# A down product in quarters, attention scores in column tiles, and the second quantisation's factor on GpSimd

## What is computed

```python
def _act_quant(x):
    scale = 127.0 / jnp.clip(jnp.max(jnp.abs(x), axis=-1, keepdims=True), 0.0001, None)
    y = jnp.clip(jnp.round(x * scale), -128, 127) / scale
def _ternary_quant(w):
    s = jnp.mean(jnp.abs(w))
    wq = jnp.round(jnp.tanh(w / (s + EPS))) * jnp.arctanh(s)
def _linear_bit(x, w, g):
    return einsum('bsd,od->bso', _act_quant(_rmsnorm(x, g)), _ternary_quant(w))

x = x + xattn(_layernorm(x), ctx, mask)        # softmax over 64 context rows
u = _layernorm(x)
h = silu(_linear_bit(u, w1, g1)) * _linear_bit(u, w2, g2)   # inner width 2048
x = x + _linear_bit(h, w3, g3)
```

## Time and profile before

| what | value |
|---|---|
| median of 3 runs | 471.52 us (470.7 to 474.17) |
| the profiled execution's own time | 472.33 us |
| its span, first to last instruction | 470.5 us |
| PE busy | 409.9 us, 87% of the span |
| VectorE busy | 407.1 us, 87% |
| GpSimd busy | 341.3 us, 73% |
| ScalarE busy | 339.5 us, 72% |
| mean granted TensorE clock | 0.942 of full speed |

### The profile page before, as it was taken

The page is one execution under the profiler, slowest core; times in us unless marked ns, Lnnn a source line. Parts: engine busy times, 40 slices in busy tenths (PEclk is TensorE's granted clock), DMA queues, the critical chain, the costliest instruction groups (busy, mean ns, idle before and its releaser), DMA issues. The chain is left out here.

```text
span 470.5 us, 8445 instructions
## 1 busy us (share of the span) xinstructions
PE 409.9 (87%) x1966; PEld 197.5 (42%) x1966; DVE 407.1 (87%) x927; ACT 339.5 (72%) x607; POOL 341.3 (73%) x539
## 2 busy tenths in 40 slices
PE   8326644899999999999999999999999999999995
PEld 8102412344644464446434543445444634334432
DVE  3799576889899999999999999999999999999662
ACT  1585446986798769886988788878886796666552
POOL 0267858787777787788788787778777877878650
PEclk9756795899999999999999999999999999999998
DMA  7999901545557455745574466447654444444431
GB/s 270 396 366 421 312 16 22 135 90 114 139 148 173 90 114 143 179 88 115 165 178 89 111 182 163 90 111 189 139 129 111 91 88 91 86 94 91 90 69 45
DMA packets 110504, 67.45 MB, mean 143 GB/s; under 512 B 100752, under 2 KB 100880, under 8 KB 106768
## 3 DMA queue, kind: packets, MB, share of 16 engines
q1 hardware_dynamic: 110480, 67.19, 53.9%
HBM read 34.14 MB, written 8.39 MB: 90 GB/s over the span
## 5 line engine op out<-in xcount | busy, mean ns | idle before, releaser
L521 POOL TENSOR_TENSOR stageB<-stageB,g3b 128x512 f32<-128x512 f32 x128 | 163.8, 1285 | 46.2 <-DVE stageB L907 45.3
L1163 PE MATMUL S<-W2q,q12T 128*128 128x512 f16 x512 | 134.5, 386 | 8.9 <-DVE stageB L907 6.2
L1163 PE MATMUL S<-W1q,q12T 128*128 128x512 f16 x512 | 135.3, 388 | 0.0
L693 ACT ACTIVATE sg<-S,asc 128x512 f32<-128x512 f32 x128 | 87.5, 683 | 54.1 <-PE S L1163 49.3
L1191 PE MATMUL DN<-W3q,stageB 128*128 128x512 f16 x512 | 118.7, 386 | 7.3 <-DMA stageB<-stageB 7.3
L907 DVE TENSOR_TENSOR stageB<-sg,S 128x512 f32<-128x512 f32 x128 | 86.7, 677 | 19.9 <-ACT sg L693 10.5
L913 DVE TENSOR_REDUCE hm<-stageB 128x1 f32<-128x512 f32 x128 | 86.5, 677 | 0.2 <-POOL stageB L521 0.2
L1163 PEld LDWEIGHTS S<-W2q,q12T 128*128 128x128 f16 x512 | 49.5, 99 | 75.3 <-DVE stageB L907 13.9
L1191 PEld LDWEIGHTS DN<-W3q,stageB 128*128 128x128 f16 x512 | 49.8, 99 | 70.3 <-issue 10.8
L1163 PEld LDWEIGHTS S<-W1q,q12T 128*128 128x128 f16 x512 | 49.8, 100 | 66.3 <-issue 10.1
L685 ACT ACTIVATE stageB<-stageB,hf 128x1024 f16<-128x1024 f32 x64 | 69.8, 1140 | 4.8 <-DVE hf L933 4.8
(11 more groups left out here) (112 smaller groups left out, 430.7 us busy)
## 6 DMA issues: line engine op xcount, KB each, us to landing
xTs<-in_xT SPq DMA_DIRECT2D x8, 1024.0 KB, 7.0
X<-in_x SPq DMA_DIRECT2D x8, 1024.0 KB, 6.0
out_x<-X SPq DMA_DIRECT2D x32, 256.0 KB, 2.9
X<-in_w1T SPq DMA_DIRECT2D x4, 1024.0 KB, 12.5
stageB<-in_w2T SPq DMA_DIRECT2D x4, 1024.0 KB, 20.4
X<-in_w3T SPq DMA_DIRECT2D x4, 1024.0 KB, 9.2
ctxr<-in_ctx SPq DMA_DIRECT2D x16, 128.0 KB, 3.1
ctxc<-in_ctx SPq DMA_DIRECT2D x8, 128.0 KB, 3.9
```

The costliest lines, as they stand in the source:

```text
L521: nc.gpsimd.tensor_tensor(gh[q][:, part], hp[:, part], g3b[:, part], ALU.mult).then_inc(s_gh_made, 1)
L693: nc.scalar.activation(sg[n % 2][:, :], S1[n % 2][:, :], ACT.Silu, scale=asc[z][:, 0:1])\
L1163: mm = nc.tensor.matmul(bank[n % 2][:, :], q12T[q][:, i * KD + k, :], w[:, n, k, :], start=(k == 0), stop=(k == KD - 1))
```

## The change

Four things are changed together.

1. The down product of tile t - 2 is cut in quarters of 4 matmuls and spread over the slot: one after up chunk 0, one after chunk 1, two after chunk 2. A new semaphore `s_down_top` says that the upper half of q3T has been read, and the first transpose of the next tile waits for that instead of the whole product.
2. The scores are computed the other way round: the centred context ccT (128 x 64) is the weight, and 256 columns of x transposed are moved; even tiles go to columns 0 to 63 of the array and odd tiles to columns 64 to 127 (`tile_position`). The result lies transposed in PSUM; ScalarE copies it to the new tile `half`, and two PE transposes turn it back before the softmax.
3. stage_h_factor and worth_3 move from VectorE to GpSimd, four operations. VectorE keeps the maximum and takes the reciprocal of it directly. On GpSimd the root and the factor stand behind stage_a_mean and quantize_12 of the new row instead of before them.
4. `result` on VectorE moves from before gate 1 or 2 to between max_3(t, 0) and gate 3, and `hsc` has two buffers.

In the diff, subscripts of whole tiles and unchanged waits are dropped.

```diff
 def load_xT(a):
-    sp.wait_ge(s_scores_ps, a)
+    sp.wait_ge(s_half_ps, a)
 def transpose_3(t, h):
-    sp.wait_ge(s_down_ps, t)
+    sp.wait_ge(s_down_ps if h else s_down_top, t)
 # gpsimd
+def stage_h_root(t, z):
+    ...
+    tensor_scalar(hkk, hk, asc[z][:, 1:2], QMAX * QUANTUM / ACT_MAX_FLOOR, mult, mult)
+def stage_h_factor(t):
+    pool.wait_ge(s_h_kk, t + 1)
+    pool.wait_ge(s_h_r, t + 1)
+    ...
+    tensor_scalar(hf, hr, QMAX * QUANTUM, hkk, mult, min)
+    ...
+    tensor_scalar(ha, hm1, hkk, QMAX * QUANTUM, mult, max)
+def worth_3(t, q):
+    pool.wait_ge(s_h_a, t + 1)
+    tensor_scalar(hsc[q], ha, wc[:, 2:3], ACT_MAX_FLOOR / (QMAX * QUANTUM), mult, mult)
 slot, gpsimd:
     gain_3(t - 1, 3, (j - 1) % 2)
-    stage_h_root(t - 1, (j - 1) % NZ)
     stage_a_mean(t + 2, (j + 2) % TPB)
     quantize_12(t + 1)
+    stage_h_root(t - 1, (j - 1) % NZ)
+    stage_h_factor(t - 1)
+    worth_3(t - 1, (j - 1) % 2)
     stage_a_worth(t + 1, (j + 1) % NZ)
 # scalar
+def attention_half(a):
+    act.wait_ge(s_half_ps, a + 1)
+    nc.scalar.copy(half[:, :], R[1][:, 0:TPB // 2 * P]).then_inc(s_half_made, 1)
 slot, scalar:
 silu(t, 1, j % NZ)
 if attn and j == 0 and not first:
+    attention_half(b + 1)
     two(x_square, b + 1, 2)
 # vector
 def stage_h_top(t):
     tensor_reduce(hm1, hm, AX_X, max).then_inc(s_h_max, 1)
+    dve.wait_ge(s_h_max, t + 1)
+    reciprocal(hr, hm1).then_inc(s_h_r, 1)
 # tensor
 def attention_scores(a):
-    for j in range(TPB):
-        for k in range(KD):
-            matmul(R[1][:, j * M:(j + 1) * M], xTs[:, k, j, :], ccT[:, k, :], ...)
+    for k in range(KD):
+        for e in range(2):
+            matmul(R[1][e * M:(e + 1) * M, 0:TPB // 2 * P], ccT[:, k, :], xTs[:, k, e::2, :],
+                   ..., tile_position=(0, e * M))
+def attention_turn(a):
+    pe.wait_ge(s_half_made, a + 1)
+    for i in range(TPB // 2):
+        transpose(R[1][:, i * P:(i + 1) * P], half[:, i * P:(i + 1) * P], identf)
 slot, tensor:
 up(t, 0, q)
-down(t - 2)
+down(t - 2, 0, 1)
 up(t, 1, q)
+down(t - 2, 1, 1)
 if attn and j == 0: attention_scores(a)
 up(t, 2, q)
+down(t - 2, 2, 2)
+if attn and j == 0: attention_turn(a)
 up(t, 3, q)
```

More of the change, by code:

```diff
@@ L107, in bit_ffn_xattn @@
         identf = sb("identf", [P, P])
+        half = sb("half", [P, TPB // 2 * P])
         warm = sb("warm", [P, 4])
@@ L153, in bit_ffn_xattn @@
         hkk = sb("hkk", [P, 1])
-        ha = [sb(f"ha{i}", [P, 1]) for i in range(2)]
+        ha = sb("ha", [P, 1])
         hr = sb("hr", [P, 1])
         hf = sb("hf", [P, 1])
-        hsc = sb("hsc", [P, 1])
+        hsc = [sb(f"hsc{i}", [P, 1]) for i in range(2)]
         S1 = [ps(f"S1_{i}", [P, CH]) for i in range(2)]
@@ L597, in slot @@
                     quantize_12(t + 1)
+                if not (first and j == 0):
+                    stage_h_root(t - 1, (j - 1) % NZ)
+                    stage_h_factor(t - 1)
+                    if not (first and j == 1):
+                        worth_3(t - 1, (j - 1) % 2)
+                if not (last and j == TPB - 1):
                     if first and j == 0:
@@ L1040, in slot @@
                     stage_a_gain(t + 2)
-                if not early and j == 1:
-                    worth_3(t - 2, j % 2)
-                    result(t - 2)
                 gate(t, 1)
@@ L1052, in slot @@
                     weight_scale(2, stageA, W3f, 1, s_w3_dve)
-                if not early and j != 1:
-                    worth_3(t - 2, j % 2)
-                    result(t - 2)
                 if attn and j < 3:
                     stage_a_max(t + 2)
-                if first and j == 1:
-                    stage_h_factor(0, 0, 0)
                 gate(t, 2)
@@ L1067, in slot @@
                     weight_clip(W3f, 1, s_w3_dve, 1, s_w3_q)
+                if not early:
+                    result(t - 2, j % 2)
                 gate(t, 3)
@@ L1211, in slot @@
                     attention_ccT(a)
-                if not (first and j < 2):
-                    down(t - 2)
+                turn = not (first and j < 2)
+                if turn:
+                    down(t - 2, 0, 1)
                 up(t, 1, q)
+                if turn:
+                    down(t - 2, 1, 1)
                 if attn and j == 0:
@@ L1226, in slot @@
                 up(t, 2, q)
+                if turn:
+                    down(t - 2, 2, 2)
                 if first and j == 0:
                     attention_scores(a)
+                if attn and j == 0 and not first:
+                    attention_turn(a)
                 up(t, 3, q)
+                if first and j == 0:
+                    attention_turn(a)
                 if attn and j == 1:
@@ L1236, in _ @@
             turn_3(NT - 1)
-            down(NT - 1, True)
+            down(NT - 1, turned=True)
 def kernel(**inputs):
```

101 lines of the change are left out of this document (59 added, 42 removed).

## The result

The changed kernel takes **477.24 us** (median of 5 runs, 475.9 to 477.92) against 472.18 for the kernel before on the same chip (470.7 to 474.17): a ratio of **1.0104, interval 1.0071 to 1.0137**. It is slower by about 5 us where I forecast 11 faster; the time lies above my range. The loss is clear of the scatter, but the interval holds the 1% that I had called the least a measurement can tell. Ranges and ratios in this document are of executions at the kernel's usual granted clock; one execution further down, at a mean clock of 0.927 where the same kernel's others had 0.943 to 0.945, stands outside them.

The account below looks back on a forecast made before the run. VectorE and PE were taken to bound the middle together. Gains of 7.8 (six batches), 2.0 (batch 7), 1.2 (batch 0) and 0.2 (end) sum to 11.2 us: 460.3 on the median, range 453 to 470, the forecast's own 456 to 465.

Parts of the forecast that it names:

- What bounds before: Middle batches: VectorE (49.2 us occupied) and PE (48.3) bound together, VectorE slightly first; GpSimd occupies 42.4.
- Change 3 on GpSimd: Four one-element operations added on GpSimd: 1.3 us a slot, 5.3 a batch, raising its occupied time from 42.4 to 47.7.
- the stretch exists in each slot already: GpSimd beside VectorE's gains: stretching only moves to other operations and is already in the 42.4, so 1.3 a slot holds.
- The allowance for waits: Middle batches: 0.5 us for waits between nearly equally full engines, giving 48.2 a batch, 1.3 less than 49.50.
- my slower rival: GpSimd waits for the new row's mean, 1.35 us in three of four slots: 51.75 a batch, 481.6 us; 7%.
- Change 2 on PE: Scores on PE fall from 3.51 us to 2.3, plus 0.3 for two transposes; PE goes from 48.3 to 47.4 a batch.
- Change 1 and batch 7: Batch 7: the 1.1 us late transpose is covered by 1.7 of PE work; 2.0 of 3.3 us of waits gained.
- hf now stands behind the new row's 1.36: GpSimd's chain is late next after the transpose wait goes, as hf follows 1.36 us of the new row's quantising.
- The start and the end: Batch 0 gains 1.2 us because c comes earlier on VectorE; the end gains 0.2 as two small operations change engine.
- The rule on the shared port pair: VectorE and GpSimd block each other fully: at most 0.9 us a slot more on GpSimd; forecast kept 1.3 a slot.
- that rival: GpSimd stands for VectorE's whole 1.67 us gain pair: 51.3 a batch, 478.9 us, 3%; at half, 468.1, 5%.
- The two slower rivals: GpSimd waiting at its slot's new head (481.6 us, 7%) and standing for the whole gain pair (478.9 us, 3%).

Follow-up runs that it names:

- the first experiment: Kernel before with changes 1, 2 and 4 but the factor left on VectorE and GpSimd's order unchanged: 462.87 us, ratio 0.9789.
- the kernel with the root first: Changed kernel with the inner row's root and hkk put back ahead of the new row's mean on GpSimd: 470.22 us, ratio 0.997 to the kernel before.

## Why the prediction was wrong, point by point

**What bounds before.** Right. With changes 1, 2 and 4 alone the loop stays at 49.4, because VectorE is full. And the change did relieve VectorE: 6.4 us of waits for other engines in a batch, from 0.2.

**Change 3 on GpSimd: the term that failed.** I had 42.4 + 5.3 = 47.7; it occupies 49.4, 1.7 more. The busy column gives 4.6 of the 7.0 that were added, the latency between small operations the other 2.4. The undisturbed price is 1.59 a slot, not 1.3: from start to start hkk has 0.47, hf 0.29, ha 0.48 and hsc 0.35, where I took the pace of one dependent pair, 0.37, for three and 0.2 for ha. That is 1.2 of the 1.7 a batch. The rest, 0.5, is the sentence "the stretch exists in each slot already": the power operation of the new row is no longer stretched (0.57, from 0.94), but hk, hkk, hf and ha, which have taken its place beside VectorE's gains, lose more together: about 2.3 in this batch beyond their undisturbed times, where ak and hk lost about 1.6 before. I had seen the upper bound, 2.9 a slot, and kept it only for the range of an unlikely rival. Counting all of an engine's new latency as occupied was right: one more operation cost 0.32 each time.

**The allowance for waits: the second miss.** I allowed 0.5 a batch; the mean costs 1.5, in slot 2 of each batch. I had argued that the fullest engine runs late. It does run late into three of the slots; in slot 2 it is done with its gains at 343.21 and the mean cannot start before 344.73. That is the mechanism of my slower rival (GpSimd waits at the new head of its slot), in one of its three places, and the kernel with the root first is without it. 1.7 + 1.0 = 2.7 is the whole of 50.9 against 48.2. Over batches 1 to 6, 50.77 on the mean, this makes 15.4; with 1.7 for batch 7 and 1.4 less for the start it is 15.7, the distance from the span that I forecast, 470.5 - 11.2 = 459.3, to 475.0.

**Change 2 on PE.** The mechanism was right, the tiles overlap; the size was 0.5 too dear (2.1 with the turn for 2.6); in particular no row had priced the 0.2 for another shape of the array. It is worth nothing alone, 1.0029.

**Change 1 and batch 7.** The mechanism was right alone: in the first experiment the wait for the DMA was gone. That batch 7 fell by 2.1 there, beside my 2.0, is luck: I had worked out 2.0 as what GpSimd with change 3 would leave of 3.3. It was wrong in the sum, the third miss: with change 3, PE still waits 3.4 us for the DMA, against 4.4, and the batch gives 0.3, not 2.0. I named the successor, "hf now stands behind the new row's 1.36", and then priced the batch by GpSimd's amount alone. What is late is not the engine but its output: hf comes after c, and quantising and the transpose hang on it. ScalarE's waits for hf in batch 7 are 6.9 us in four times, and were 2.4 in one. The runs with and without change 3 put this on change 3; whether its order or its length does it in batch 7 was not tried by itself.

**The start and the end.** 2.6 and 0.3 for 1.2 and 0.2; the first is within the scatter of the start.

**The rule on the shared port pair.** I set the row (0.39 of delay beside a pair of 1.67) above the rule of the Trainium skill (SBUF — State Buffer, two separate sides: the pair is an "exclusive lock"). The rows here agree with the rule more than with my reading, and they show one such delay in a slot, where my sum for that rival took off two: hf and ha each end with one of VectorE's two gains; VectorE's operation of 0.48 takes 1.37 and ends after GpSimd's gain has. In the forecast the row was a mean case and I used it as the price. By the rule the extra is at most what remains of the operation that came first, so it depends on who is late. The price that I had missed was mostly something else: 1.2 of the 1.7 a batch are the pace of the small operations themselves.

**The chances.** The two slower rivals had 10% together. Their arithmetic was in the right place; what happened was a third of the one and a part of the other at the same time, and I had treated them as alternatives to a forecast with hardly a width of its own.

## What to carry to other kernels

When work is moved from a full engine to one with a few microseconds of room, price each small operation on its new engine from a chain of the same shape, its latency included, and compare the sum with the room before looking at what is saved: here 7 us of waits a batch had to take 7.0 of new work and an order that opened a wait. A part of a change that relieves engine A can be worth nothing while B is full, so the price of each part is best told by the kernel without it. In a ring of engines, look at where an operation stands more than at how long it is: the same VectorE operation, moved within its slot, was worth 14 us by the two ratios.

## What the runs showed of the hardware

Two products of 64 columns of weights in float32, on the two column halves of the array, run beside each other: 8 products of 256 columns in 1.88 us, starting in pairs. An operation of one element a partition on GpSimd holds it for 0.32 to 0.48 us when it depends on the one before. Of 0.29 to 0.32 alone, it took up to 0.88 beside an operation of VectorE with two operands in SBUF and ended 0.1 to 0.2 after that one; and a VectorE operation from float32 to float16, 0.48 alone, took 0.70 to 1.37 beside GpSimd's gains, ending 0.28 or 0.29 after them. In these rows it is a stall for what is left of the other's operation, in both directions, so a GpSimd that is early can pay more of it than one that is late.
